# Edge loop of a graph-attention layer: another order for two kinds of scatter, a later load, and earlier quantisation

## The reference, cut to what matters

```python
N, E, HEADS, D = 625, 10000, 8, 64
h_e = einsum('nf,hfd->hnd', x, W_e)
h_r = einsum('nf,hfd->hnd', x, W_r)
diff = h_r[:, dst] - h_r[:, src]
score = (s_src + s_dst + einsum('hed,hd->he', diff, a_dif)
         + einsum('hed,hd->he', abs(diff), a_abs)
         + einsum('hed,hd->he', h_r[:, src] * h_r[:, dst], a_prd))
alpha = leaky_relu(score, 0.2)
ex = exp(alpha - segment_max(alpha, src)[src])
att = ex / (segment_sum(ex, src)[src] + 1e-16)
out = segment_sum(att * h_e[:, dst], src)
...
scale = mean(abs(w_group_of_128)) + 1e-5
wq = clip(round(w_group_of_128 / scale), -1, 1) * scale
x = x + (silu(x @ wq_gate.T) * (x @ wq_up.T)) @ wq_down.T
```

## Time and profile before

| what | value |
|---|---|
| median of 3 runs | 2196.59 us |
| the profiled execution, its own time | 2197.39 us |
| its span | 2195.6 us |
| PE busy | 2077.8 us, 95% |
| DVE busy | 1041.9 us, 47% |
| ACT busy | 724.6 us, 33% |
| POOL busy | 557.2 us, 25% |
| idle time of PE ahead of L904 (edge loop) | 24.1 us |
| mean granted TensorE clock | 0.98 |

### The profile page before, as it was taken

The page is one execution under the profiler, slowest core; times in us unless marked ns, Lnnn a source line. Parts: engine busy times, 40 slices in busy tenths (PEclk is TensorE's granted clock), DMA queues, the critical chain, the costliest instruction groups (busy, mean ns, idle before and its releaser), DMA issues.

```text
span 2195.6 us, 21978 instructions
## 1 busy us (share of the span) xinstructions
PE 2077.8 (95%) x8164; PEld 1261.8 (57%) x8164; DVE 1041.9 (47%) x2151; ACT 724.6 (33%) x1226; POOL 557.2 (25%) x475
## 2 busy tenths in 40 slices
PE   6998898799999999999999999999999999999998
PEld 3575565688666655545665665665565444444443
DVE  8886767787664433474543554454345200000002
ACT  2576655677432200032432432342241111111110
POOL 4577774443320100112022012003002200122202
PEclk9999999799999999999999999999999999999999
DMA  9622211831021111111011011011010877777822
GB/s 343 196 31 30 30 14 36 218 92 61 33 86 59 58 67 42 39 63 68 10 63 68 10 58 69 13 58 63 0 58 28 306 278 301 295 296 302 300 108 76
DMA packets 61524, 237.49 MB, mean 108 GB/s; under 512 B 23351, under 2 KB 28427, under 8 KB 39292
## 3 DMA queue, kind: packets, MB, share of 16 engines
q1 hardware_dynamic: 31914, 168.27, 21.4%
q0 software_dynamic: 26336, 62.19, 9.3%
q10 hardware_dynamic: 3168, 5.63, 0.7%
HBM read 204.07 MB, written 31.96 MB: 108 GB/s over the span
## 4 chain that ended last, share of the span: by engine, by line
PE 74%; DVE 13%; issue 5%; DMA 3%; POOL 2%; ACT 2%; PEldq 0%; PEld 0%; ACTq 0%; DVEq 0%; SPq 0%; POOLq 0%
PE PS L759 10%; PE PS L752 10%; PE PS L1054 10%; PE PS L1485 7%; PE PS L1494 7%; PE PS L1523 7%; PE PS L1097 2%; PE PS L1364 2%; PE PS L1281 2%; DMA pair_scores<-TS,SIDX 2%; PE PS L904 2%; PE PS L1384 2%; PE PS L1385 2%; POOL pair_scores L2105 2%; PE PS L1263 1%
## 5 line engine op out<-in xcount | busy, mean ns | idle before, releaser
L2075 POOL TENSOR_TENSOR RSTD<-VE,HALF 125x1 f32<-125x1 f32 x100 | 81.4, 814 | 943.8 <-DVE VE L2246 943.8
L1054 PE MATMUL PS<-XT,WR 128*128 128x500 f32 (+2 forms) x992 | 232.1, 391 | 8.5 <-ACT XT L1591 3.5
L904 PE MATMUL PS<-HR,HOT 125*125 125x512 f32 x800 | 211.8, 413 | 24.1 <-DVE HOT L2392 24.1
L3132 DVE TENSOR_TENSOR AR<-AR,PS 128x512 f32<-128x512 f32 (+1 forms) x44 | 30.2, 687 | 404.6 <-PE PS L1494 402.3
L759 PE MATMUL PS<-WR,XT 128*125 128x512 f32 x424 | 194.6, 606 | 0.9 <-DVE AR L2909 0.9
L1054 PEld LDWEIGHTS PS<-XT,WR 128*128 128x128 f32 x992 | 143.8, 191 | 86.7 <-issue 70.6
L904 PEld LDWEIGHTS PS<-HR,HOT 125*125 125x125 f32 x800 | 146.8, 191 | 66.8 <-DVE HOT L2392 26.1
L2094 POOL DMA_INDIRECT pair_sums<-CW,SIDX x80 | 136.5, 1706 | 52.6 <-DMA pair_sums<-CW,SIDX 27.0
L759 PEld LDWEIGHTS PS<-WR,XT 128*125 128x125 f32 x424 | 79.0, 192 | 87.0 <-issue 83.4
L2035 ACT ACTIVATE AR<-PS 128x512 f32<-128x512 f32 (+1 forms) x44 | 26.3, 597 | 299.1 <-PE PS L1485 299.1
L752 PE MATMUL PS<-XT,WR 128*128 128x313 f32 (+3 forms) x432 | 122.8, 441 | 1.3 <-DVE CW L2356 0.8
(11 more groups left out here) (457 smaller groups left out, 3918.1 us busy)
## 6 DMA issues: line engine op xcount, KB each, us to landing
WR<-in_qkv SPq DMA_DIRECT2D x12, 1024.0 KB
WR<-in_omm SPq DMA_DIRECT2D x12, 1024.0 KB
pair_scores<-CNT SPq DMA_DIRECT2D x1, 12212.0 KB
AR<-pair_scores SPq DMA_DIRECT2D x5, 2187.5 KB
AR<-in_x_a SPq DMA_DIRECT2D x10, 1024.0 KB, 9.8
AR<-in_x_b SPq DMA_DIRECT2D x10, 1024.0 KB, 5.0
AR<-in_x_c SPq DMA_DIRECT2D x10, 1024.0 KB, 7.2
WR<-in_x_a SPq DMA_DIRECT2D x8, 1024.0 KB, 9.2
```

What stands on the lines that cost most here:

```text
L904: last = mm(DIFF[m % 4], HOT[g % 2][0:P, k, tile(j)], HR[0:P, k, :, b, :], start=(k == 0 and b == 0), stop=(k == NT - 1 and b == 1))
L1054: last = mm(by_tile(s)[:, t0:t1, :], w[:, k, 128 * m:128 * (m + 1)], XT[:, k, P * t0:P * t1].rearrange("p (c n) -> p c n", n=P), start=(k ...
L2075: g.tensor_tensor(RSTD[:, t:t + 1], VE[:, t:t + 1], HALF[:, :], ALU.pow)\
```

## The change

It has five parts, all in the order of work; no instruction is added or taken away.

- POOL: 16 sums first (LEAD), then each score scatter followed by a share of 54 sums, then ten sums (SUMS_BEHIND).
- SP: the load of the first third stands after the edge rows of group 10. After the loop the scores of tile 0 are read before the sums of tile 0, and the wait for all sums stands between the two.
- ACT: the quantisation waits for the last score instead of for uv_ready 5.
- DVE: the factors (L2486, L2489) come after the second quantised group, and the join (L2535) after the fourth.
- The merges come later. On DVE merge(0) stands after raw score 3 and the others at steps 0, 1, 3 and 6; on POOL all five stand after products 2, 3, 4, 6 and 8.

```diff
-LEAD = 20
+LEAD = 16
+SUMS_BEHIND = 10
...
@@ loads(sp) @@
-            sp.wait_ge(uv_ready, 1)
-            load([mat(1, 0, "gate", 0), mat(1, 1, "up", 0), mat(1, 2, "down", 0)])
-
             sp.wait_ge(hr_split, NT)
...
                     sp.wait_ge(edge_read, g - 3)
                     edge_rows(g)
+                if g == 10:
+                    sp.wait_ge(uv_ready, 1)
+                    load([mat(1, 0, "gate", 0), mat(1, 1, "up", 0), mat(1, 2, "down", 0)])
...
-            for b in range(2):
-                sp.wait_ge(sums_scattered[b], 16 * ET // 2)
...
+            sp.wait_ge(diff_filled, ET)
+            sp.wait_ge(scattered, 16 * ET)
+            scores_of(0)
+            for b in range(2):
+                sp.wait_ge(sums_scattered[b], 16 * ET // 2)
             sp.wait_ge(edge_read, GROUPS)
             sp.wait_ge(graph_filled, 1)
             sums_of(0)
-            sp.wait_ge(diff_filled, ET)
-            sp.wait_ge(scattered, 16 * ET)
-            scores_of(0)
             sp.wait_ge(scaled_ready, 1)
             sums_of(1)
             sums_of(2)
@@ ACT @@
-            act.wait_ge(uv_ready, 5)
+            act.wait_ge(score_ready, ET)
             ahead = quantized(0)
@@ POOL @@
-            for m in range(ET + LEAD):
-                if m < ET:
-                    add_sums(m)
-                if m >= LEAD:
-                    put_scores(m - LEAD)
+            among = ET - LEAD - SUMS_BEHIND
+            for m in range(LEAD):
+                add_sums(m)
+            for m in range(ET):
+                put_scores(m)
+                for s in range(LEAD + m * among // ET, LEAD + (m + 1) * among // ET):
+                    add_sums(s)
+            for m in range(ET - SUMS_BEHIND, ET):
+                add_sums(m)
...
-            merge(0)
...
-                if k in (0, 1, 4, 7):
-                    merge((0, 1, 4, 7).index(k) + 1)
+                if k in (2, 3, 4, 6, 8):
+                    merge((2, 3, 4, 6, 8).index(k))
@@ DVE @@
             for t in range(NT):
                 psum.skip(T=2)
                 next(ahead)
+                if t == 1:
+                    spread_factors()
+                if t == 3:
+                    dve.wait_ge(graph_taken, 1)
+                    for k, part_ in enumerate((EA1[0:DH0, :], PS[0:DH0, 2 * BANK:2 * BANK + N])):
+                        v.tensor_tensor(EA2[0:DH0, :], EA2[0:DH0, :], part_, ALU.add).then_inc(graph_joined, 1)
+                        dve.wait_ge(graph_joined, k + 1)
...
-            merge(0)
             for k in range(4):
                 raw_scores(k)
                 shift(k)
-                if k % 2:
-                    merge(1 + k // 2)
+            merge(0)
...
-                if k in (1, 6):
-                    merge(3 + k // 6)
+                if k in (0, 1, 3, 6):
+                    merge((0, 1, 3, 6).index(k) + 1)
```

More of the change, by code:

```diff
@@ L2480, in _, with spread_factors @@
             dve.wait_ge(score_ready, ET)
-            step(v.tensor_scalar(UP[:, :, :], U[:, :, :], -0.8, None, ALU.mult))
-            for lo in (0, DH0):
-                rows = slice(lo, lo + DH0)
-                v.tensor_tensor(
-                    SPREAD[rows, :, :].rearrange("p h (b d) -> p h b d", b=2),
-                    ID[rows, rows].unsqueeze(1).unsqueeze(1).broadcast_to([DH0, HEADS0, 2, DH0]),
-                    PRODUCT[rows, :].unsqueeze(2).unsqueeze(3).broadcast_to([DH0, HEADS0, 2, DH0]),
-                    ALU.mult).then_inc(uv_ready, 1)
+            def spread_factors():
+                step(v.tensor_scalar(UP[:, :, :], U[:, :, :], -0.8, None, ALU.mult))
+                for lo in (0, DH0):
+                    rows = slice(lo, lo + DH0)
+                    v.tensor_tensor(
+                        SPREAD[rows, :, :].rearrange("p h (b d) -> p h b d", b=2),
+                        ID[rows, rows].unsqueeze(1).unsqueeze(1).broadcast_to([DH0, HEADS0, 2, DH0]),
+                        PRODUCT[rows, :].unsqueeze(2).unsqueeze(3).broadcast_to([DH0, HEADS0, 2, DH0]),
+                        ALU.mult).then_inc(uv_ready, 1)
             def quantized(u):
@@ L2520, in _ @@
             ahead = quantized(0)
-            dve.wait_ge(graph_taken, 1)
-            for k, part_ in enumerate((EA1[0:DH0, :], PS[0:DH0, 2 * BANK:2 * BANK + N])):
-                v.tensor_tensor(EA2[0:DH0, :], EA2[0:DH0, :], part_, ALU.add).then_inc(graph_joined, 1)
-                dve.wait_ge(graph_joined, k + 1)
             for t in range(NT):
```

## The result

The changed kernel takes **2212.79 us** (median of 12 runs, 2202.28 to 2216.66), the kernel before, run beside it, 2199.16 us (12 runs, 2192.53 to 2211.56): a ratio of 1.0047, 95% interval 1.0031 to 1.0064. It is 0.47% **slower**. (This isn't the ratio of the two medians, which is 1.0062; the means, 2210.6 and 2200.4 us, give 0.47% too.) Forecast were 2191.9 us and a range up to 2204. The profiled execution took 2211.59 us (span 2209.8), 14.2 us more than that of before.

The account below looks back on a forecast made before the run. From 180 us on, POOL's scatter queue was taken to set the edge loop's pace; L is the end of the last score. -13.5 there and +8.8 given back make -4.7: 2196.6 to 2191.9 us, range 2180 to 2204.

Parts of the forecast that it names:

- the second rival: After the edge loop: pair sums arrive too late and the loop's gain is lost; 2202.9 us, chance 0.18.
- the place at head 8: Raw score 8, which waits for the scores of tile 1: the mechanism by which late sums lose the loop's gain.
- a last sum later than L + 53.5: On POOL, 53.5 us after the last score: beyond this, tile 1's scores land too late and the loop's gain is lost.
- the clock: Granted clock after the loop: longer idling could cost 0 to 3 us; charged 0, as waits replace existing ones.
- Order of the scatters and load: Edge loop on POOL: fewer sums first, load at the tenth group; last score at 344.2, 13.5 us sooner.
- The load's +5: Edge loop: delay of POOL's scatters by the load at the tenth group, taken as 5 us, bounds +1 and +8.
- Quantisation sooner: After the last score: quantisation starts 2.9 us sooner, first raw scores at about L + 38.3 instead of L + 39.4.
- The 1.1 us: First raw scores: the gain expected from the sooner quantisation, said to go into the next wait.
- Scores first, sums last: POOL behind the last score: eleven sums left, 3.7 us each beside the scores' read; the last lands near L + 49.
- The next scores: Read of tile 1's scores: done by L + 78.7, so raw score 8 gives back 8.8 us; bounds 3 and 13.
- What would show it wrong: Signs: PE's one-hot waits stay, scatters beside the load wait none or several over 5 us, or raw score 8 isn't waited for.
- its list of right ones: Signs: last score near 344, one-hot waits under 10 us, sums ending near L + 49, DMA waits, raw score 8 near 423.

Follow-up runs that it names:

- e9: The changed kernel itself run once more, unaltered: 2210.8 us against 2200.16 for the kernel before, ratio 1.0049.
- e2: The changed kernel with the load of the first third back at its old place: 2201.08 us, ratio 1.002 to the kernel before.
- e5: The kernel before with only the load moved to the tenth group of edges: 2200.34 us against 2198.59, ratio 1.0004.
- e10: The kernel before with 16 sums first, one behind each of score scatters 0 to 63, and the load at the tenth group: 2197.76 us, ratio 0.9971.
- e4: The kernel before with the sooner quantisation alone, factors after the second group and join after the fourth: 2198.54 us, ratio 0.9995.
- e3: The changed kernel with the scores of tile 0 read only when all sums have landed: 2219.03 us, ratio 1.0076 to the kernel before.
- e1: The changed kernel with no sums behind the score scatters (SUMS_BEHIND = 0): 2205.51 us against 2197.36 for the kernel before, ratio 1.0033.
- e11: The kernel before with 16 sums first, one behind each of score scatters 0 to 63, and the change's reads and merges: 2203.87 us, ratio 1.001.
- e8: The changed kernel with 55 identity transposes on TensorE ahead of its wait for the merged counts: 2209.49 us (6 runs), ratio 1.0049.
- e12: The same kernel as e8 run once more, against the kernel before: 2211.88 us (10 runs), ratio 1.0057.
- e6: The changed kernel with no sums behind the last scatter and reads and merges in the old order: 2201.35 us against 2198.59, ratio 1.0017.
- e7: The kernel before with only 16 sums first instead of 20, then one behind each of score scatters 0 to 63: 2189.64 us, ratio 0.9956.

## Why the prediction was wrong

The direction was wrong, and it is the second rival that came: "the place at head 8", with its point at "a last sum later than L + 53.5". The last sum started at L + 54.1 and landed near L + 57. Rival 2 gave 2202.9, and the nine runs of the change at an undisturbed clock have 2203.0. That agreement is luck: its terms were a loop gain of 5.7 and 12.0 given back, measured were 14.6 and 21.0. Two terms of the sum failed, the last sum (L + 49 forecast, L + 57 measured) and the read of the next scores (9.9 us forecast, 13.9 measured), and a third, the clock, was put at nothing. Step by step:

- **Order of the scatters and load**: 344.2 was forecast for L, with -13.5. Measured 343.1 (-14.6), 341.5 in e9. Scatter 0 at 99.56 (100.4 forecast), PE's one-hot waits 7.6 (under 10). Right. The load's +5 fits two waits of 4.76 and 2.10, and the 3.8 to 6.5 us by which L differs in e2, e5 and e10; since equal loops differed by 10 from one execution to another, the size is not shown more closely than that. By the rule of the Trainium skill (DMA: Bandwidth & Descriptors, Queues, rings and completion order) on turns between queues it would be +1. Of the load the trace leaves that open, since the two waits in e5 are only 5.2 us together and something of each is there without it; of the scores' read it doesn't agree (next point).
- **Quantisation sooner**: L + 38.3 forecast, L + 39.9 measured, no effect in e4. The 1.1 us never came.
- **Scores first, sums last**: here the sum failed. "Beside it I take 3.7 us each, three until L + 36" was a mean over a stall. In the change the sums don't run slower beside the read one by one; one of them waits 10.95 us, until the read's bytes are through, and the rest go at 1.85 afterwards. In e2 it is two waits, of 4.77 and 5.12, with the second ending after the read as well. The 5.93 us of the earlier trace rows was such a stall, and it was halved by spreading it over two sums. By the forecast five sums were started by L + 36, when the read ends, and six were left; in truth two were started when the wait ended, at 382.38 = L + 39.3, and nine were left. Three more sums of 1.85 are 5.5 us, the later end of the wait 3.3: together 8.8, of the 8 us from L + 49 to L + 57 (the forecast also gave the last sum a little more time to land). e3 (no read beside the sums, no stall), e1 (a single sum in flight stalls as well) and e9 (the same stall again) show it.
- **The next scores**: L + 49 + 4 x 5.0 + 9.9 = L + 78.7 was the forecast (it adds up to 78.9), measured L + 90.9. The four reads of sums went as forecast: issued from 400.23 on, with the scores of tile 1 behind them at 420.13, 19.9 us later, L + 77.0. That is 8 of the 12 us, all of it the late sums. The other 4 are the length of the read of the scores. The forecast gave it 2.5 MB / 252 GB/s = 9.9 us; from issue to raw score 8 it took 433.99 - 420.13 = 13.9, at a rate that was no lower (254 GB/s in 421 to 431). The rest is the time ahead of the first byte, about 1 us, and about 3 from the last byte to the use. e11 has 13.7 for the same read.
  The release was misread too: scores_of(1) went when VectorE's third merge behind k = 1 was done (418.34 + 1.76 = 420.10), and the text looked at POOL's behind product 4 alone, which ended at 419.4. In the change that cost about nothing, since the reads of the sums had only just ended; with early sums, in e11, that merge is what holds the read.
- **The clock**: "I charge 0, because these waits replace waits that are there now". The reason was wrong: the wait before merge(0) is a new one (PE idle 15.46 us), and the clock falls to 0.50 there. Low stretches later in the program come in 15 of 24 runs and carry some 6 of the 10 us between the means. After the 12 us at raw score 8 this is the second largest error.
- **What would show it wrong**: the text named PE's one-hot waits, scatters beside the load, and raw score 8. None of them came: the one-hot waits fell, two scatters waited 4.76 and 2.10, and raw score 8 was waited for. The signs that counted stood on its list of right ones, the end of the eleven sums "near L + 49" and raw score 8 "near 423", and there the run was 8 and, at 433.99, 11 us off. That every stage from head 8 on would be as long as before didn't come either.

What stays open: what decides when a low stretch comes. e8 and e12 filled the wait and were as slow as the change, and e11 has low clocks in a third of its runs without a late sum; that the idle time *causes* them is suggested by the counts (23 of 40 runs in the change, e2 and e3; 13 of 98 before), but no run shows the link within one execution, and e6 and e1 have 3 of 10 with short waits.

## What to carry to other kernels

A small scatter next to a bulk read doesn't have to share with it in proportion: here one stood until the read was over, and what was queued behind it on its engine with it. So put the scatters well ahead of the read, as the kernel before and e7 do, and price one that is left beside it by the length of the whole read; holding the read back until they have landed cost more (e3). Price a read from its issue to its first use, not by its bytes over the rate: here that was 13.9 us and not 9.9. When an order is changed to bring one event forward, follow the first buffer that is freed by the moved work (here the one for tile 1's scores, three merges away) before counting a gain. And where two streams share an engine, start the one that others wait for as soon as its first item is there: e7's first score scatter started 11.6 us sooner, and that carries its gain.

## What the runs showed of the hardware

- Beside a read of 2.5 MB POOL waited 10.95, 10.85, 10.94 and 10.95 us for a scatter of 125 rows to land (the change, e9, e8, e12), and 0.3 without the read (e3). The read itself wasn't slowed: 251 GB/s in 370 to 379, where the earlier trace rows has 252 for a read of the same array, then nothing in 379 to 382. In e2 the wait came in two parts, 4.77 and 5.12. The Trainium skill's rule on turns between queues (DMA: Bandwidth & Descriptors, Queues, rings and completion order) would let the scatter through after a packet or so; the trace doesn't agree, or the time goes elsewhere than into waiting for a turn, which no run here tells apart.
- A read of 2.5 MB whose bytes moved in 10 us took 13.9 us from its issue to the instruction that waited for it (13.7 in e11).
- The mean granted clock of a run goes with its time: 98 runs of one kernel lie at 2198.3 us above 0.973 and at 2212.1 at or below it. One execution therefore can't price a change of 5 us. Sorting the runs by clock helps within one kernel; between kernels the bound can differ, as e7's run of 2202.5 us at 0.974 and e12's of 2208 to 2214 at 0.974 show.
